# A decoder's first cross attention: query-key products in three float32r passes, stationary values in 64-column tiles with a turn back, maxima over two heads at once, row sums from a column of ones

## What is computed

```python
q = _qdq(x) @ _qdq(wq).T + bq
kv = cond @ wkv.T + bkv
k, v = jnp.split(kv, 2, axis=-1)
...
scale = 1.0 / np.sqrt(Dh)
attn = jax.nn.softmax(jnp.einsum('bnhd,bmhd->bhnm', q, k) * scale, axis=-1)
o = jnp.einsum('bhnm,bmhd->bnhd', attn, v).reshape(B, N, C)
out = _qdq(o) @ _qdq(wp).T + bp
```

## Time and profile before

| | us |
|---|---|
| median of 3 runs | 2807.86 (2807.6 to 2813.41) |
| span of the profiled execution | 2808.8 |
| PE busy | 2598.3 (93%) |
| DVE busy | 1717.6 (61%) |
| ACT busy | 1129.9 (40%) |
| POOL busy | 764.2 (27%) |

### The profile page before, as it was taken

The page is one execution under the profiler, slowest core; times in us unless marked ns, Lnnn a source line. Parts: engine busy times, 40 slices in busy tenths (PEclk is TensorE's granted clock), DMA queues, the critical chain, the costliest instruction groups (busy, mean ns, idle before and its releaser), DMA issues. The chain is left out here.

```text
span 2808.8 us, 49906 instructions
## 1 busy us (share of the span) xinstructions
PE 2598.3 (93%) x15563; PEld 2142.5 (76%) x15564; DVE 1717.6 (61%) x3341; ACT 1129.9 (40%) x2434; POOL 764.2 (27%) x791
## 2 busy tenths in 40 slices
PE   8999799979899999799996998989999999899998
PEld 7888677768688777578875876767777788788887
DVE  4537767669777666576665576864444435656564
ACT  2103255523343324455543233755444421444343
POOL 3213100024333235423233101740000012345455
PEclk9999999999899979899997998999999989999999
DMA  5454122125622045477773432353212031666664
GB/s 191 152 144 99 36 87 73 45 73 162 175 73 63 17 145 188 141 216 219 197 225 86 127 71 75 117 174 91 87 49 87 8 129 58 164 158 150 159 150 82
DMA packets 289285, 332.98 MB, mean 119 GB/s; under 512 B 147446, under 2 KB 202694, under 8 KB 287313
## 3 DMA queue, kind: packets, MB, share of 16 engines
q1 hardware_dynamic: 217904, 252.57, 28.8%
q0 software_dynamic: 20640, 51.74, 9.3%
q10 hardware_dynamic: 50560, 26.34, 3.2%
HBM read 233.86 MB, written 96.72 MB: 118 GB/s over the span
## 5 line engine op out<-in xcount | busy, mean ns | idle before, releaser
L898 PE MATMUL e_psum<-e_up_hi,hT_hi 128*128 x672 | 246.8, 367 | 21.3 <-DVE hT_lo L867 12.7
L900 PE MATMUL e_psum<-e_up_hi,hT_lo 128*128 x672 | 238.1, 354 | 0.0
L899 PE MATMUL e_psum<-e_up_lo,hT_hi 128*128 x672 | 238.0, 354 | 0.0
L898 PEld LDWEIGHTS e_psum<-e_up_hi,hT_hi 128*128 128x128 f32 x672 | 128.7, 192 | 43.8 <-issue 32.4
L1565 POOL TENSOR_TENSOR self_a_p<-self_a_p,self_a_mx 112x448 f32<-112x448 f32 x96 | 96.0, 1000 | 205.2 <-DVE self_a_mx L1622 205.2
L794 ACT ACTIVATE e_gate<-e_psum 128x352 f32<-128x352 f32 (+1 forms) x86 | 44.4, 516 | 260.1 <-PE e_psum L900 256.0
L873 DVE TENSOR_TENSOR hT_lo<-e_psum,hT_hi 128x256 fp32r<-128x256 f32 (+2 forms) x138 | 55.7, 435 | 143.4 <-ACT hT_hi L812 135.6
L1656 ACT ACTIVATE self_a_p<-self_a_p 112x448 f32<-112x448 f32 x128 | 71.6, 575 | 165.0 <-POOL self_a_p L1565 113.9
L900 PEld LDWEIGHTS e_psum<-e_up_hi,hT_lo 128*128 128x128 f32 x672 | 128.6, 191 | 11.7
L899 PEld LDWEIGHTS e_psum<-e_up_lo,hT_hi 128*128 128x128 f32 x672 | 128.8, 192 | 9.9
L1786 PEld LDWEIGHTS joint_psum<-x_v,joint_a_pt 125*112 125x112 f32 (+1 forms) x1024 | 120.1, 179 | 19.8 <-issue 14.4
(11 more groups left out here) (563 smaller groups left out, 7385.1 us busy)
## 6 DMA issues: line engine op xcount, KB each, us to landing
e_up_raw<-in_L_ffn_w SPq DMA_DIRECT2D x64, 512.0 KB, 4.9
e_up_raw<-in_L_ffn_w SPq DMA_DIRECT2D x64, 352.0 KB
e_dn_raw<-in_L_ffn_w SPq DMA_DIRECT2D x16, 1024.0 KB, 15.0
q_all<-p_p_t_stage ACTq DMA_DIRECT2D x56, 256.0 KB
e_dn_raw<-in_L_ffn_w SPq DMA_DIRECT2D x16, 512.0 KB
x_q<-q_all SPq DMA_DIRECT2D x8, 896.0 KB
v_ctx<-front_c_v_stage SPq DMA_DIRECT2D x24, 250.0 KB
x_others<-k_ctx SPq DMA_DIRECT2D x8, 750.0 KB, 4.7
```

What stands on the lines that cost most here:

```text
L898: pe.matmul(out, lhs[0], rhs[0], start=k == 0, stop=False)
L899: pe.matmul(out, lhs[0], rhs[1], start=False, stop=False)
L900: return pe.matmul(out, lhs[1], rhs[0], start=False, stop=k == n_k - 1)
```

## The change

A new class `HeadCrossPart` takes the place of `CrossAttentionPart` in cross1 (the last cross attention keeps the old class).

- **Scores.** Queries and keys are split into a high and a low float32r part, and a head's scores are three float32r products of 376 columns (high x high, high x low, low x high) instead of one float32 product. Sequence 0 is split at the start of the segment on ScalarE and VectorE, in five pieces each; every later one during the sequence before: high parts on ScalarE at its step 3, low parts on GpSimd at its step 4.
- **Banks.** The two heads' scores lie in neighbouring PSUM banks, with two such pairs of banks; one maximum over both banks (112x2), one negation, and one copy of both heads' transposed probabilities (125x672).
- **Values.** They are stored with 33 columns a head, the last of them ones. 64 columns from a head's first are stationary, the transposed probabilities (112 columns) move, and two heads write the upper and the lower 64 partitions of one bank. This is done for four heads at once, at every second step. The result (features x tokens) is copied to SBUF (128x224, ScalarE), turned back by two transposes on TensorE in the next step, and VectorE takes the reciprocal of the column of sums from PSUM and scales. The exponentials leave no row sums any more.
- `v_stage`, the DRAM copy (`v1_ctx`) and the loads have 528 columns instead of 512; GpSimd sets the ones once. The norm part and its order are unchanged, but its phases begin two half-steps later, since the attention's lead is 6 instead of 4.

```diff
+class HeadCrossPart:
...
+        n_heads, dh, W, GROUP = 16, 32, 2, 4
+        E, CP = dh + 1, C + C % 2
+        n_steps, per_batch = n_heads // W, n_heads // GROUP
+        n_all = B * n_steps
+        PAIRS, PT, LT, LP, LE, O_RING = 3, 4, 2, 2, 3, 3
+        BACK = 2 * T
...
+        def s_bank(at):
+            return s_banks[2 * (at % 2)]
...
+        def gpsimd(pool):
...
+                if b < B and n == 4:
+                    u = b % 2
+                    pool.wait_ge(hi_ready, 2 * b - 1)
+                    pool.tensor_tensor(q_lo[:, u, :, :], q_raw[:, u, :, :], q_hi[:, u, :, :].bitcast(F32), ALU.subtract).then_inc(lo_ready, 1)
+                    pool.wait_ge(hi_ready, 2 * b)
+                    pool.tensor_tensor(k_lo[:, u, :, 0:C], k_raw[:, u, :, :], k_hi[:, u, :, 0:C].bitcast(F32), ALU.subtract).then_inc(lo_ready, 1)
...
+        def tensor(pe):
+            yield
+            yield
+            for step in range(n_all + LE):
+                at = pair(step, LT)
+                if at is not None:
+                    pe.wait_ge(exp_done, W * at + W)
+                    reuse(pe, pt_ready, at)
+                    for u in range(W):
+                        for c in range(CCH):
+                            last = pe.transpose(ps[0:CT, t_banks[u], c * T:(c + 1) * T], p[:, (W * at + u) % (PAIRS * W), c * CT:(c + 1) * CT],
+                                                core.ident[0:T, 0:T])
+                    last.then_inc(t_done, 1)
+                at = pair(step)
+                if at is not None:
+                    b, h0 = at // n_steps, W * (at % n_steps)
+                    if b == 0:
+                        if at == 0:
+                            pe.wait_ge(padded, 2)
+                        pe.wait_ge(first_lo, 2 + h0 // 4)
+                    elif h0 == 0:
+                        pe.wait_ge(lo_ready, 2 * b)
+                    reuse(pe, exp_done, W * (at - 1))
+                    for part, (q_part, k_part) in enumerate(((q_hi, k_hi), (q_hi, k_lo), (q_lo, k_hi))):
+                        for u in range(W):
+                            h = h0 + u
+                            rows = slice(h % 4 * dh, (h % 4 + 1) * dh)
+                            last = pe.matmul(ps[0:T, s_bank(at) + u, 0:CP], q_part[rows, b % 2, h // 4, :], k_part[rows, b % 2, h // 4, :],
+                                             start=part == 0, stop=part == 2)
+                    last.then_inc(s_done, 1)
+                done = group_of(step, LE)
+                if done is not None:
+                    pe.wait_ge(ot_ready, done + 1)
+                    for x in range(2):
+                        last = pe.transpose(ps[0:T, o_bank, BACK + x * 128:BACK + (x + 1) * 128], ot[:, x * T:(x + 1) * T], core.ident[:, :])
+                    last.then_inc(back_done, 1)
+                yield
+                made = group_of(step, LP)
+                if made is not None:
+                    b = made // per_batch
+                    if made % per_batch == 0:
+                        reuse(pe, v_in[b % 2], (b // 2 + 1 - int(b % 2 == 0)) * 16 * CCH)
+                    pe.wait_ge(pt_ready, 2 * made + 2)
+                    reuse(pe, o_evac, made)
+                    for x in range(2):
+                        for c in range(CCH):
+                            for r in range(2):
+                                j = 2 * x + r
+                                first = (GROUP * (made % per_batch) + j) * E
+                                last = pe.matmul(ps[64 * r:64 * r + 64, o_bank, x * T:(x + 1) * T], v[0:CT, b % 2, c, first:first + 64],
+                                                 pt[0:CT, (GROUP * made + j) % PT, c, :], start=c == 0, stop=c == CCH - 1)
+                    last.then_inc(pv_done, 1)
...
+        def vector(dve):
+            dve.wait_ge(first_hi, 1)
+            dve.tensor_tensor(q_lo[:, 0, :, :], q_raw[:, 0, :, :], q_hi[:, 0, :, :].bitcast(F32), ALU.subtract).then_inc(first_lo, 1)
+            for c in range(4):
+                dve.wait_ge(first_hi, c + 2)
+                dve.tensor_tensor(k_lo[:, 0, c, 0:C], k_raw[:, 0, c, :], k_hi[:, 0, c, 0:C].bitcast(F32), ALU.subtract).then_inc(first_lo, 1)
+            yield
...
+                    rs = slice(W * (at % PAIRS), W * (at % PAIRS) + W)
+                    dve.wait_ge(s_done, at + 1)
+                    reuse(dve, exp_done, W * (at - PAIRS + 1))
+                    dve.tensor_reduce(mx[:, rs], ps[0:T, s_bank(at):s_bank(at) + W, 0:C], AX.X, ALU.max).then_inc(mx_ready, 1)
+                    dve.wait_ge(mx_ready, at + 1)
+                    dve.tensor_scalar(neg[:, rs], mx[:, rs], -scale, None, ALU.mult).then_inc(neg_ready, 1)
...
+                done = group_of(step, LE)
+                if done is not None:
+                    unit, part = done // per_batch, done % per_batch
+                    back = ps[0:T, o_bank, BACK:BACK + GROUP * 64].rearrange("p (h e) -> p h e", h=GROUP)
+                    dve.wait_ge(back_done, done + 1)
...
+                    dve.reciprocal(rinv[:, done % 2, :], back[:, :, dh]).then_inc(rinv_ready, 1)
+                    dve.wait_ge(rinv_ready, done + 1)
+                    dve.tensor_tensor(o[:, unit % O_RING, part * GROUP * dh:(part + 1) * GROUP * dh].rearrange("p (h d) -> p h d", h=GROUP),
+                                      back[:, :, 0:dh], rinv[:, done % 2, :].unsqueeze(2).to_broadcast([T, GROUP, dh]), ALU.mult).then_inc(o_evac, 1)
...
+        def scalar(act):
...
+            for step in range(n_all + LE):
+                b, n = step // n_steps + 1, step % n_steps
+                at = pair(step, LT)
+                if at is not None:
+                    act.wait_ge(t_done, at + 1)
+                    reuse(act, pv_done, (at - 2) // 2 + 1)
+                    slots = W * at % PT
+                    src = ps[0:CT, t_banks[0]:t_banks[0] + W, 0:CCH * T].rearrange("p u (c t) -> p u c t", c=CCH)
+                    act.copy(pt[0:CT, slots:slots + W, :, :], src).then_inc(pt_ready, 1)
+                if b < B and n == 3:
+                    u = b % 2
+                    act.wait_ge(qk_in[u], 32 * ((b + 1) // 2))
+                    reuse(act, s_done, (b - 1) * n_steps)
+                    act.activation(q_hi[:, u, :, :], q_raw[:, u, :, :], ACT.Copy).then_inc(hi_ready, 1)
+                    act.activation(k_hi[:, u, :, 0:C], k_raw[:, u, :, :], ACT.Copy).then_inc(hi_ready, 1)
+                yield
+                at = pair(step)
+                if at is not None:
+                    act.wait_ge(neg_ready, at + 1)
+                    reuse(act, t_done, at - PAIRS + 1)
+                    for x in range(W):
+                        r = W * (at % PAIRS) + x
+                        act.activation(p[:, r, :], ps[0:T, s_bank(at) + x, 0:C], ACT.Exp, bias=neg[:, r:r + 1], scale=scale).then_inc(exp_done, 1)
+                made = group_of(step, LP)
+                if made is not None:
+                    act.wait_ge(pv_done, made + 1)
+                    reuse(act, back_done, made)
+                    act.copy(ot[:, :], ps[:, o_bank, 0:2 * T]).then_inc(ot_ready, 1)
...
-        v_stage = g.sb(f"{name}_v_stage", [CT, CCH, D])
+        v_stage = g.sb(f"{name}_v_stage", [CT, CCH, D // 32, 33])
+            pool.memset(v_stage[:, :, :, 32:33], 1.0).then_inc(ones_set, 1)
-                    dve.tensor_tensor(v_stage[:, c, :], ps[0:CT, v_banks[c], :], b_row[:, :], ALU.add).then_inc(v_ready, 1)
+                    dve.tensor_tensor(v_stage[:, c, :, 0:32], ps[0:CT, v_banks[c], :].rearrange("p (h d) -> p h d", d=32),
+                                      b_row[:, :].rearrange("p (h d) -> p h d", d=32), ALU.add).then_inc(v_ready, 1)
...
+        v1_ctx = core.dram("v1_ctx", [B, CCH, 128, D // 32 * 33])
-                    a = CrossAttentionPart(g, "a", 32, lambda b: q1[b], lambda b: [(slice(0, C), k_ctx[b])],
-                                           lambda b: [v_ctx[b, c, 0:CT, :] for c in range(CCH)], [CT] * CCH, 32.0 ** -0.5,
-                                           (0, 1, 2), (3, 4), (5, 6), 2, tiles=(q1_t, k1_t, v1_t))
+                    flat_q = wq[:, :, :].rearrange("p k d -> p (k d)")
+                    q1_split = [flat_q[:, part * 8 * T:(part + 1) * 8 * T].rearrange("p (u c t) -> p u c t", u=2, c=4) for part in range(2)]
+                    a = HeadCrossPart(g, "a", lambda b: q1[b], lambda b: k_ctx[b], lambda b, c: v1_ctx[b, c, 0:CT, :], 32.0 ** -0.5,
+                                      (0, 1, 2, 3), (4, 5), 6, (q1_t, k1_t, v1_t), q1_split)
```

88 lines of the change are left out of this document (81 added, 7 removed).

## The result

| kernel | median us (runs) | ratio to before [95% interval] | span | clock of the whole run |
|---|---|---|---|---|
| before | 2810.23 (2807.6 to 2813.41, 4) | | 2808.8 | 0.953 |
| after | 2844.29 (2843.59 to 2845.36, 4) | 1.0125 [1.0113, 1.0137] | 2841.9 | 0.94 |

What follows compares the result with a forecast made beforehand. TensorE bounds a plain step before; after, a chain through ScalarE and VectorE does. Loop -3.8, norm part -6.3, start +2.5, end +1.5 sum to -6.1 us on 2808.8, giving 2802 us; range 2778 to 2838.

Steps and rivals of the forecast that it cites:

- TensorE's own work: TensorE's busy time in two plain steps of cross1: 4.59 us after the change, 5.90 before.
- the loop of two steps: Closed chain from values' block through scores, maximum, exponentials and copy back: 5.78 us for two steps, 3.8 us saved overall.
- the pairs of halves and of scores: On TensorE, two 64-column halves run at once, 0.098 us a pair; two heads' score products at once, 0.172.
- a TensorE-bound pair: Rival: the chain is shorter, TensorE stays the bound, two steps fall towards 4.59 us, 2770 in all; chance 0.13.
- halves or scores one after another: Two rivals: values' halves run singly, 2839 us, chance 0.14; score products run one head at a time, 2818, chance 0.08.
- The norm part, 3.5 us a sequence: Norm work adds 3.5 us a sequence instead of 4.4; over seven sequences -6.3 us.
- The second delay: Two steps after the eight products, VectorE's queue of 7.25 us makes the next maximum 1.5 us late.
- GpSimd's low parts ... Nothing.: Low parts on GpSimd, 4.4 us from step 4, needed at step 8, 11 us later: no cost.
- The clock: A granted clock below 0.96 in the stretch was named only as a sign of being wrong, outside the sum.
- The splits on ScalarE; loads: High parts at step 3, about 0.5 + 1.455 us off the loop, and earlier key and query loads: no cost.
- Start, +2.5 us: Before the first maximum, five copies on ScalarE and five subtractions on VectorE: +2.5 us.
- End, +1.5: At the end, a whole pair's copy for the last values' block, an output copy and a turn back: +1.5 us.

Runs made afterwards that it cites:

- e11: Changed kernel with float32 scores and no splits, VectorE's scaling right behind the negation, four filler products ahead of most values' blocks: 2805.4 us.
- e1: Changed kernel with the low parts of the splits made on VectorE instead of GpSimd: 2824.4 us.
- e5: e4 plus four unused full-height products ahead of three values' blocks in four: 2812.7 us.
- e4: e1 with VectorE's scaling of a group's output moved right behind the negation, ahead of the norm part's operations: 2829.9 us.
- e6: e4 plus the unused filler products in the first sequence alone: 2831.5 us.
- e8: Changed kernel with float32 scores, no splits, untiled values products in every step with 33 moving columns, no turn back, heads copied one by one: 2927.7 us.
- e12: e8 with 128 moving columns in the values products instead of 33, outputs 42 columns apart: 2804.9 us.
- e13: e12 with three unused copies on ScalarE ahead of the real ones in every second step: 2823.0 us.
- e15: e12 with five unused copies on ScalarE ahead of the real ones in every second step: 2859.7 us.
- e17: e14 with the low parts on GpSimd instead of VectorE: 2821.7 us.
- e14: e12 with three-pass scores and their splits, low parts on VectorE: 2806.3 us.
- e2: Changed kernel with five unused full-height products on TensorE ahead of each values' block: 2847.7 us.
- e3: Changed kernel with both edits, low parts on VectorE (e1) and five full-height filler products (e2): 2832.4 us.

## Why the prediction was wrong, step by step

- **TensorE's own work, the loop of two steps, the pairs of halves and of scores.** Right, each within 0.1 us: the pair 5.86 for 5.78, the values' block 1.30 for 1.37, the maximum 0.94 for 0.94, the copy 0.72 for 0.72. The rivals of a TensorE-bound pair and of halves or scores one after another all fall. The estimate from the Trainium skill, "TensorE: Matmul & The Clock Gate", section "Measured speedup vs the span model", 0.12 a pair, would give the values' block 1.63; it took 1.30. The 0.095 for a row of 112 columns stands in none of the rows shown; four transposes at 444.60 of the kernel before have 0.097, those of the earlier trace rows 0.109.
- **The norm part, 3.5 us a sequence.** Right where clock and splits are out of the way: e11's sequences of 27.4 to 27.5 us are four pairs of 5.95 and 3.6 to 3.7. The eight products' pair takes 7.8, 1.9 more, against 2.0 forecast. The second delay has the forecast size (1.5 us in e1, 7.3 for 5.8) but another last link: not the next maximum but the scaling that frees the output bank.
- **"GpSimd's low parts ... Nothing."** This step failed: moving them off GpSimd makes the segment 10.3 us shorter (after to e1) and the whole kernel 20. I asked when they are needed and who waits for them (11 us of slack, nobody), not what runs beside them on VectorE. On VectorE they are not free either: e5's sequence is 28.0, with plain pairs 0.13 shorter than e11's, so they cost some 1.1 a sequence, 8 us.
- **The clock.** This step failed too. The sum took every row at full speed and named a lower clock only among what would show it wrong; the stretch had 0.79. Between e1 and e5 lie 12 us, 14.8 in the segment, and e5 still has the early scaling, which by itself cost 4 to 6 (e4). The loop was forecast to leave 1.2 us of waiting in every pair, and that this has a price beyond itself is missing from the sum.
- **The splits on ScalarE; loads.** Nothing, as said.
- **Start, +2.5 us.** Right: the first maximum comes 5.02 us behind the last VectorE row of self0 (357.67, 352.65) against 2.76 before (352.78, 350.02), +2.3. What the sum lacks is the clock behind it: half speed lasts to 385, against 363 before. Filler won some 3 us of that back (e6); the rest is open.
- **End, +1.5.** From the last values' block to the next segment's first product 21.4 us for 18.9, +2.6, at a clock of 0.58 for 0.73.
- **Front.** Nothing, as said: the additions into `v_stage` take 692 ns for 689.

The account, in the segment: 250.6 - 6.1 = 244.5 forecast; 8 for the low parts on any engine and 1 for the end, both worked out; 14.8 for the clock and 10.3 for GpSimd's hold, both differences of single profiled executions: 278.6, against 282.6 measured. 4 us are open. e5 still runs part of the segment at half clock, and its filler has a cost of its own. The whole kernel missed by 42 us, 38 of them in this segment.

## What to carry to other kernels

Where a change turns a TensorE-bound loop into one in which TensorE waits in every round, its clock can be part of the price: look at the granted clock, and whether filling the waits with unused products makes the kernel faster (17 us here). Measure the changed segment by itself as well as the whole: of the 20 us that e1 gained only 10 lay in it. Work moved to GpSimd with tiles in SBUF on both sides is to be laid against VectorE's SBUF instructions in the same microseconds, not against its own deadline. And fewer moving columns in small products may save nothing: 33 for 128 took the same row time within a tenth, and the clock fell from 0.95 to 0.55.

## What the runs showed of the hardware

- A busy TensorE stayed near half clock by the form of its products alone: 98% busy and 0.55 with 33 moving columns in the values' block, 0.95 with 128, all else but the outputs' spacing equal (e8, e12).
- Waits of 0.74 us in pairs of 6.7 left the clock alone, waits of 1.43 in pairs of 7.4 lowered it in short pieces (e13, e15).
- Two 64-column halves in float32 ran side by side: 24 rows in 1.30 us, the change of tile among it, where one after another, at the 0.097 of four transposes with the same 112 columns (0.55 us with the last one's 0.26, before, 444.60), they would take 2.3.
- Beside GpSimd's subtractions a negation of 112x2 took 2.10 us for 0.17 (e17), and a quantise of 112x512 3.27 for 0.43 (after). The hold cost 10.3 us in the changed kernel's segment, 14.0 and 21.6 where the waits on TensorE were shorter or filled (e17 and e14, e2 and e3).
